# A Mamba round laid out anew on four engines: where the read-outs, the silu calls, the D term and the output product stand

## The chip, the cores and the metric

The kernel runs on one core of a Trainium2 chip. A core has TensorE (PE, matrix products), VectorE (DVE), ScalarE (ACT), GpSimd (POOL) and SyncE (SP), which here issues nearly all transfers. Each engine works through a queue of its own in order, and they wait for one another on semaphores. The metric is the device time of one execution in microseconds (us). Before the change three runs took 8188.65, 8215.14 and 8237.64 us, a median of 8215.14 us.

## What is computed

A decoder of two layers on 64 sequences of 128 tokens with 128 features, in float32. The part that the change touches is the first one, a Mamba model of four layers with 256 inner channels and 16 states each. One layer is, cut to what matters:

```python
hidden = _layernorm(residual, norm_w[i], norm_b[i])
xz = einsum('bld,ed->ble', hidden, in_w)
xin, z = split(xz, 2)
xc = silu(_causal_conv(xin, cw, cb))
dbc = einsum('bld,ed->ble', xc, xp_w)          # dtr (8), Bm (16), Cm (16)
dt = softplus(einsum('blr,dr->bld', dtr, dtp_w) + dtp_b)
# for each token t, from h = 0:
h = exp(dt[t, :, None] * A) * h + (dt[t] * xc[t])[:, None] * Bm[t]
y[t] = einsum('dn,n->d', h, Cm[t])
y = (y + xc * D) * silu(z)
residual = residual + einsum('bld,ed->ble', y, out_w)
...
```

The parts behind it (a cross attention, a layer of experts, a trajectory layer, a decoder layer and a quantized feed-forward layer) run later in the same program and stay as they are.

## The kernel before

`mamba_stage` works in rounds. A round handles four sequences (512 tokens) of one layer; there are 16 rounds a layer and 4 layers. Channels lie on the partitions, in two halves, so a state of one round is a tile of 128 x 1024 (two halves, four sequences, 128 tokens). `round_of` is one round: a block with one queue for each engine, written out by hand, then a barrier at the block's end, then `s.clear()`, in which SP clears all of the stage's semaphores and a second barrier holds all engines. The 16 states n of a round are a pipeline over four engines:

- ScalarE makes the decay factors of state n into PSUM (`act_da`: zeros for each sequence's first token, L347, and two exponentials, L350), one state ahead; PSUM holds them for two states.
- GpSimd makes the products dBu (`pool_dbu`, L365) into a ring of four tiles, three states ahead.
- VectorE runs the recurrence of state n over the tokens (`dve_scan`, L379). For eleven states it then multiplies with C (`dve_read_out`, L393, into `hcd`); for the five states of `ON_POOL` (1, 5, 8, 10, 13) the scan goes into `hs`, and GpSimd multiplies (`pool_read_out`, L402, into `hcp`).
- TensorE adds these products up in two PSUM banks, by a product with the identity (`pe_sum`, L419). The sums begin with the D term (`pe_skip`, L407).

Woven in between are three other things. `Behind` ends the round before: its last sum (L291), the gate with silu(z) on VectorE (L296), the output product with the old residual (L300, L304), and its copy on ScalarE (L310), which SP stores. `Ahead` makes what the next round needs: the conv (L206) and its silu (L212), the x product (L217, copied at L222 and sent through DRAM, so that the B and C rows come back on all partitions), dt (first product L234, Abs and Exp at L239 and L241, a polynomial and a logarithm for softplus, L245 to L260, a second product L234, and VectorE's dt at L265), dtu on GpSimd (L270), and the z product (L275) with its silu (L280). `Pre` normalizes the tokens of the round after that: statistics on VectorE (L166, L169), the addition of eps and the sign (L171, L172), the power -0.5 on GpSimd (L176, L178), the application on ScalarE (L183), transposes on TensorE (L190), and L195.

The order on each engine is set by the text of `round_of` alone: its loops run over n, and an `if n == ...` puts an extra step behind state n. In an engine's queue a wait holds all that stands behind it.

## Time and profile before

| | us |
|---|---|
| median of three runs | 8215.14 (8188.65 to 8237.64) |
| the profiled execution, its own time | 8205.62 |
| span of its profile | 8203.8 |
| Mamba rounds within the span | about 109 to 4090 |
| VectorE busy in them | 3616 |
| GpSimd busy in them | 3349 |

The profile shows one execution. Its times count from the start of the span. Busy time is time in which an engine executes an instruction that computes or loads a table; idle time ahead of an instruction is put down to the engine that released it. TensorE's clock is granted in two levels, 2.4 GHz (1.00) and 1.2 GHz (0.50).

### The profile page before, as it was taken

The page shows a single profiled execution, that of the slowest core. Times are in us where ns is not written, and L with a number is a line of the kernel's source. Part 1 is how long each engine was busy: PE and PEld are TensorE (multiplying, and loading weights), DVE is VectorE, ACT ScalarE, POOL GpSimd, SP SyncE. Part 2 cuts the span into 40 slices and gives each one's busy share as a digit, 9 for nine tenths or more (in the row PEclk, how much of TensorE's full clock was granted, in tenths as well). Part 3 has the DMA queues.
Part 4 walks back from the last instruction along what each step waited for, and adds up shares of the span by engine and source line. Part 5 has one row for each costly group of instructions (what it writes and reads, how often), then busy time and mean ns, then how long its engine had stood idle before and what let it go on. Part 6 is the DMA issues. An engine that isn't in the chain of part 4 may idle for free. (4 is left out here: it accounts for less than half of the span.)

```text
span 8203.8 us, 93492 instructions
## 1 busy us (share of the span) xinstructions
PE 6431.1 (78%) x25989; PEld 3401.5 (41%) x25989; DVE 6477.9 (79%) x15177; ACT 4521.1 (55%) x8427; POOL 4781.6 (58%) x2957
## 2 busy tenths in 40 slices
PE   5888888888888888888788867777557777777855
PEld 2333333333333333333355545555434455555522
DVE  5999989999899998999855668898666666666557
ACT  4666666666666666666555633333324555555533
POOL 4888888888888888888732334455213333343300
PEclk9999999999999999999977878888655777777755
DMA  5333333434333343343310057777310000000011
GB/s 182 144 153 149 153 138 153 161 137 158 152 146 153 148 155 138 153 161 136 148 33 27 22 144 211 210 212 210 92 48 8 10 10 10 10 10 10 7 34 36
DMA packets 373870, 896.58 MB, mean 109 GB/s; under 512 B 28169, under 2 KB 270214, under 8 KB 307110
## 3 DMA queue, kind: packets, MB, share of 16 engines
q1 hardware_dynamic: 332646, 692.64, 22.5%
q0 software_dynamic: 40960, 201.36, 8.4%
q14 instruction: 212, 1.74, 0.1%
q8 instruction: 52, 0.85, 0.0%
HBM read 850.57 MB, written 56.77 MB: 111 GB/s over the span
## 5 line engine op out<-in xcount | busy, mean ns | idle before, releaser
L365 POOL TENSOR_TENSOR mb_dBu<-mb_dtu,mb_rows_b 128x1024 f32<-128x1024 f32 x1027 | 2402.1, 2357 | 145.0 <-POOLq L63 101.1
L379 DVE TENSOR_TENSOR_SCAN mb_bank<-mb_bank,mb_dBu 128x1024 f32<-128x1024 f32 x704 | 1610.9, 2288 | 142.7 <-PEq L63 112.1
L350 ACT ACTIVATE mb_bank<-mb_dt,mb_a_neg 128x508 f32<-128x508 f32 x2050 | 1312.7, 671 | 2.3
L419 PE MATMUL mb_bank<-mb_hcd,ident 128*128 128x512 f32 x2560 | 1211.3, 606 | 29.7 <-DVE mb_hcd L393 29.6
L419 PE MATMUL mb_bank<-mb_hcp,ident 128*128 128x512 f32 x1280 | 860.9, 810 | 345.3 <-POOL mb_hcp L402 345.3
L402 POOL TENSOR_TENSOR mb_hcp<-mb_hs,mb_rows_c 128x1024 f32<-128x1024 f32 x320 | 751.3, 2348 | 478.6 <-DVE mb_hs L379 445.6
L393 DVE TENSOR_TENSOR mb_hcd<-mb_bank,mb_rows_c 128x1024 f32<-128x1024 f32 x704 | 862.1, 1225 | 32.1 <-PE mb_bank L419 0.4
L419 PEld LDWEIGHTS mb_bank<-mb_hcd,ident 128*128 128x128 f32 x2560 | 499.1, 200 | 758.7 <-issue 632.5
L379 DVE TENSOR_TENSOR_SCAN mb_hs<-mb_bank,mb_dBu 128x1024 f32<-128x1024 f32 x320 | 731.1, 2285 | 83.5 <-ACT mb_bank L350 81.7
L1527 POOL DMA_INDIRECT ex_rows<-in_ex_table,ex_idx x512 | 490.0, 957 | 523.5 <-DVE ex_idx L1523 309.7
L419 PEld LDWEIGHTS mb_bank<-mb_hcp,ident 128*128 128x128 f32 x1280 | 306.1, 254 | 779.2 <-POOL mb_hcp L402 413.4
L1020 PE MATMUL de_bank<-ident,de_a_e 128*128 128x128 f32 (+1 forms) x2048 | 373.4, 342 | 213.3 <-DVE de_a_e L1136 213.3
L347 ACT ACTIVATE mb_bank<-mb_zeros 128x8 f32<-128x8 f32 x1025 | 176.1, 172 | 620.4 <-DVE mb_hcd L393 292.6
L206 PE MATMUL mb_bank<-mb_h_ch,mb_w_conv 128*128 128x512 f32 x1040 | 480.6, 604 | 44.0 <-ACT mb_r_post L310 44.0
L977 POOL TENSOR_TENSOR de_a_e<-de_a_sp,de_a_m 128x1024 f32<-128x1024 f32 x128 | 244.9, 1913 | 343.4 <-DVE de_a_m L1122 193.0
L1020 PEld LDWEIGHTS de_bank<-ident,de_a_e 128*128 128x128 f32 (+1 forms) x2048 | 303.8, 182 | 267.2 <-DVE de_a_e L1136 242.3
L1090 ACT ACTIVATE de_a_pt<-de_bank 128x512 f32<-128x512 f32 (+1 forms) x512 | 281.3, 591 | 124.5 <-PE de_bank L1020 124.5
L1611 ACT ACTIVATE ex_dg_in<-ident,ex_lin 128x128 f32<-128x128 f32 x512 | 156.4, 387 | 326.5 <-DVE ex_junk L1638 326.5
L1122 DVE MAX8 de_a_m<-de_a_sp 128x8 f32<-128x128 f32 x1024 | 210.0, 277 | 139.4 <-ACT de_a_sp L1075 69.2
L1504 PE MATMUL ex_bank<-ex_w_sim,ex_xT 128*128 128x512 f32 x512 | 257.7, 646 | 71.1 <-PEq L63 64.4
L206 PEld LDWEIGHTS mb_bank<-mb_h_ch,mb_w_conv 128*128 128x128 f32 x1040 | 194.0, 191 | 282.3 <-issue 226.2
L1581 PE MATMUL ex_bank<-ex_rows,ex_dg_in 128*128 128x256 f32 x1024 | 300.4, 460 | 0.0
(368 smaller groups left out, 12789.3 us busy)
## 6 DMA issues: line engine op xcount, KB each, us to landing
mb_rows_b<-bc_rows SPq DMA_DIRECT2D x259, 1024.0 KB, 7.7
mb_rows_c<-bc_rows SPq DMA_DIRECT2D x258, 1024.0 KB, 6.9
stream<-mb_r_post SPq DMA_DIRECT2D x69, 256.0 KB, 2.6
mb_r_tok<-stream SPq DMA_DIRECT2D x67, 256.0 KB, 2.7
mb_r_old<-stream SPq DMA_DIRECT2D x65, 256.0 KB, 2.8
ex_rows<-in_ex_table,ex_idx POOLq DMA_INDIRECT x512, 5.5
tj_x_tok<-stream SPq DMA_DIRECT2D x17, 256.0 KB, 3.1
bc_rows<-mb_xp SPq DMA_DIRECT2D x65, 64.0 KB, 1.6
```

Source lines behind the costliest of these rows:

```text
L206: m = nc.tensor.matmul(bank[:, M0 + c], w_conv[:, k, c * P:(c + 1) * P], h_ch[:, :, k:k + SEQ], start=(k == 0), stop=(k == DC - 1))
L350: e = nc.scalar.activation(da_of(n)[:, c * GB:(c + 1) * GB, 1:], dt[q][:, c].rearrange("p (b t) -> p b t", b=GB)[:, :, 1:], ACT.Exp, scale ...
L365: nc.gpsimd.tensor_tensor(by_c(dBu[m % RING][:]), by_c(chains(dtu[q][:])), over_c(rows_b[:, n]), ALU.mult).then_inc(s["mb_dbu"], 1)
L379: nc.vector.tensor_tensor_scan(flat(to), flat(da_of(n)), flat(dBu[n % RING][:]), 0.0, ALU.mult, ALU.add).then_inc(s["mb_scan"], 1)
L393: nc.vector.tensor_tensor(by_c(hcd[k % 3][:]), by_c(da_of(n)), over_c(rows_c[:, n]), ALU.mult).then_inc(s["mb_hcd"], 1)
L402: nc.gpsimd.tensor_tensor(by_c(hcp[k % 2][:]), by_c(hs[k % 2][:]), over_c(rows_c[:, n]), ALU.mult).then_inc(s["mb_hcp"], 1)
L419: m = nc.tensor.matmul(bank[:, B_Y + c], ident[:], part[:, c * GB:(c + 1) * GB], start=False, stop=False)
L1020: m = self.nc.tensor.transpose(self.bank[0:nk, 4 + j, h * P:(h + 1) * P], self.e_of(t, nk)[:, 4 * j + h], self.ident[:])
L1090: self.nc.scalar.activation(self.pt[t % 2][0:nk, 4 * j:4 * j + 4].rearrange("p h q -> p (h q)"), self.bank[0:nk, 4 + j], ACT.Copy).then_in ...
L1504: nc.tensor.matmul(bank[:, j], xT[q][:, b], w_sim[:, 4 * j:4 * j + 4], start=True, stop=True).then_inc(p["sim"], 1)
L1527: nc.gpsimd.indirect_dma_start(rowsb[b][:, h], None, w["table"], bass.IndirectOffsetOnAxis(idx[b][:, h:h + 1], 0)).then_inc(got[b], 16)
L1581: m = nc.tensor.matmul(bank[:, HID, 0:FI], dg_in[:, h], rowsb[k % GB][:, h, IB:IB + FI], start=False, stop=(h == PH - 1))
```

## The change

Nothing that is computed changes. In each round the order of the queues is another one:

- Semaphores: there are two sets of them (`Turns`), for even and odd rounds. SP clears the other round's set at the beginning of a round, and `s.clear()` with its barrier goes from the round's end; the block's own barrier stays.
- GpSimd makes dBu two states ahead (`AHEAD`) instead of three, and the round's own first two are made at the end of the round before. A read-out no longer stands directly behind the dBu of its state's turn but where `READ_BEHIND` puts it, behind a dBu.
- VectorE: the gate stands behind scan 1 instead of state 0, the statistics behind state 3 instead of 7, dt behind state 11 instead of 10. L171 and L172 go to ScalarE (`act_var`), behind state 5. The scaled identity for D is made in a layer's first round instead of its last.
- ScalarE: both conv silus and both halves of the z silu stand in one block behind the decay factors made at n = 2. The copy of the output product comes at n = 4.
- TensorE: the D term stands in the middle of the sums; the sums of states 13 and 15 are made at the beginning of the next round (`pe_late_sums`). The conv's first half is made at the end of the round before, the z product stands near the beginning, and the output product behind the x product. The three buffers of `hcd` are taken in the order of `HCD`.

```diff
+AHEAD = 2
+READ_BEHIND = {3: 1, 8: 5, 11: 8, 13: 10, 15: 13}
+HCD = (2, 0, 1, 2, 0, 1, 2, 0, 1, 0, 1)
...
+class Turns:
+    def clear_other(self):
+        for first, end in self.sets[1 - self.q].runs:
+            self.nc.sync.sem_clear(range(first, end))
...
                 for b in range(GB):
-                    nc.vector.bn_aggr(mv[:, b], stats[:, b])
-                dve.drain()
-                nc.vector.tensor_scalar(mv[:, :, 1], mv[:, :, 1], LN_EPS, None, ALU.add)
-                nc.vector.tensor_scalar(shift[:], mv[:, :, 0], -1.0, None, ALU.mult).then_inc(s["mb_stats"], 1)
+                    m = nc.vector.bn_aggr(mv[:, b], stats[:, b])
+                m.then_inc(s["mb_stats"], 1)
...
+            def act_var(self, act):
+                act.wait_ge(s["mb_stats"], self.turn + 1)
+                nc.scalar.activation(shift[:], mv[:, :, 0], ACT.Copy, scale=-1.0)
+                nc.scalar.activation(var[:], mv[:, :, 1], ACT.Identity, bias=eps_at[:, 0:1]).then_inc(s["mb_var"], 1)
...
             def act_z(self, act):
-                act.wait_ge(s["mb_z"], CH)
-                nc.scalar.activation(zg[self.q][:], x_psum, ACT.Silu).then_inc(s["mb_zg"], 1)
+                for c in range(CH):
+                    act.wait_ge(s["mb_z"], c + 1)
+                    nc.scalar.activation(zg[self.q][:, c], bank[:, M0 + c], ACT.Silu).then_inc(s["mb_zg"], 1)
...
-                if j >= 1:
-                    pool.wait_ge(s["mb_scan"], j)
+                if m >= RING:
+                    pool.wait_ge(s["mb_scan"], m - RING + 1)
...
                 @block.gpsimd
                 def _(pool):
-                    for n in range(DS):
-                        scan.pool_dbu(pool, n + RING - 1, n)
-                        if n in ON_POOL:
-                            scan.pool_read_out(pool, n)
-                        if n == 9:
+                    for m in range(AHEAD, DS + AHEAD):
+                        scan.pool_dbu(pool, m)
+                        if m in READ_BEHIND:
+                            scan.pool_read_out(pool, READ_BEHIND[m])
+                        if m == 13:
                             pre.pool(pool)
-                        if n == 11:
+                        if m == 14:
                             ahead.pool_dtu(pool)
...
                         scan.act_da(act, n + 1, n)
-                        if n == 1:
+                        if n == 2:
+                            for c in range(CH):
+                                ahead.act_conv(act, c, 1)
+                            act.wait_ge(s["mb_yg"], 1)
+                            ahead.act_z(act)
+                        if n == 4:
+                            ahead.act_x(act)
                             behind.act_new(act)
-                        if n == 3:
-                            for c in range(CH):
-                                ahead.act_conv(act, c)
                         if n == 5:
-                            ahead.act_x(act)
+                            pre.act_var(act)
...
                         if n == 11:
-                            ahead.act_z(act)
+                            pre.act_tokens(act)
                         if n == 12:
-                            pre.act_tokens(act)
-                        if n == 14:
...
-                        if n == 0:
+                        if n == 1:
                             behind.dve_gate(dve)
-                        if n == 6 and shape == GROUPS - 1:
+                        if n == 6 and shape == 0:
                             dve_skip(dve)
-                        if n == 7:
+                        if n == 3:
                             pre.dve(dve)
...
-                        if n == 10:
+                        if n == 11:
                             ahead.dve_dt(dve)
...
                 @block.tensor
                 def _(pe):
-                    behind.pe_last_sum(pe)
-                    ahead.pe_conv(pe, 0)
-                    behind.pe_out(pe)
...
+                    behind.pe_late_sums(pe)
+                    ahead.pe_conv(pe, 1)
+                    pe.wait_ge(s["mb_yg"], 1)
+                    scan.pe_sum(pe, 0)
+                    ahead.pe_z(pe)
+                    scan.pe_sum(pe, 1)
+                    ahead.pe_x(pe)
+                    behind.pe_out(pe, True)
+                    scan.pe_sum(pe, 2)
+                    scan.pe_sum(pe, 3)
+                    pe.wait_ge(s["mb_new"], 1)
+                    ahead.pe_dt(pe, False)
+                    for n in range(4, 10):
+                        scan.pe_sum(pe, n)
+                    ahead.pe_dt(pe, True)
+                    if shape == 0:
+                        pe.wait_ge(s["mb_skip"], 1)
+                    scan.pe_skip(pe, False)
+                    scan.pe_sum(pe, 10)
+                    scan.pe_sum(pe, 11)
+                    pe.wait_ge(s["mb_dt"], 1)
+                    pre.pe(pe)
+                    scan.pe_sum(pe, 12)
+                    pe.wait_ge(s["mb_h"], 1)
+                    following.pe_conv(pe, 0)
+                    scan.pe_sum(pe, 14)
-            s.clear()
```

GpSimd at the beginning of a round, before: `mb_hcp` is a read-out, `mb_dBu` a product, and `mb_scan` in the brackets a wait for a scan.

```order
L365 TENSOR_TENSOR mb_dBu<-mb_dtu,mb_rows_b 128x1024
L365 TENSOR_TENSOR mb_dBu<-mb_dtu,mb_rows_b 128x1024 [waits mb_scan]
L402 TENSOR_TENSOR mb_hcp<-mb_hs,mb_rows_c 128x1024 [waits mb_scan]
L365 TENSOR_TENSOR mb_dBu<-mb_dtu,mb_rows_b 128x1024 [waits mb_scan] x4
L402 TENSOR_TENSOR mb_hcp<-mb_hs,mb_rows_c 128x1024 [waits mb_scan]
L365 TENSOR_TENSOR mb_dBu<-mb_dtu,mb_rows_b 128x1024 [waits mb_scan] x3
L402 TENSOR_TENSOR mb_hcp<-mb_hs,mb_rows_c 128x1024 [waits mb_sump,mb_scan,mb_c2]
```

The same place of GpSimd's queue after:

```order
L408 TENSOR_TENSOR mb_dBu<-mb_dtu,mb_rows_b 128x1024 x2
L450 TENSOR_TENSOR mb_hcp<-mb_hs,mb_rows_c 128x1024 [waits mb_scan_0]
L408 TENSOR_TENSOR mb_dBu<-mb_dtu,mb_rows_b 128x1024 [waits mb_scan_0] x5
L450 TENSOR_TENSOR mb_hcp<-mb_hs,mb_rows_c 128x1024 [waits mb_late_0,mb_scan_0]
L408 TENSOR_TENSOR mb_dBu<-mb_dtu,mb_rows_b 128x1024 [waits mb_scan_0] x3
L450 TENSOR_TENSOR mb_hcp<-mb_hs,mb_rows_c 128x1024 [waits mb_sump_0,mb_scan_0,mb_c2_0]
```

Two products ahead of the first read-out no longer wait for a scan, and five instead of four stand between the first and the second read-out.

TensorE from the end of a round to the beginning of the next one, before (L419 and L291 are sums, L206 the conv, L300 and L304 the output product; the line with the barrier is the boundary).

```order
L419 MATMUL mb_bank<-mb_hcp,ident 128x512 [waits mb_hcp]
L419 MATMUL mb_bank<-mb_hcp,ident 128x512
L419 MATMUL mb_bank<-mb_hcd,ident 128x512 [waits mb_hcd]
L419 MATMUL mb_bank<-mb_hcd,ident 128x512
L540 UNCONDITIONAL_BRANCH
L642 UNCONDITIONAL_BRANCH [waits barrier_Pool_Activation_PE_DVE_SP_release]
L291 MATMUL mb_bank<-mb_hcd,ident 128x512 x2
L206 MATMUL mb_bank<-mb_h_ch,mb_w_conv 128x512 x4
L300 MATMUL mb_bank<-mb_r_old,ident 128x512 [waits mb_rp]
L304 MATMUL mb_bank<-mb_w_out,mb_yg 128x128 [waits mb_yg]
```

The same place after (L242 is the conv, L467 and L331 are sums, L313 the z product):

```order
L242 MATMUL mb_bank<-mb_h_ch,mb_w_conv 128x512 [waits mb_h_0]
L242 MATMUL mb_bank<-mb_h_ch,mb_w_conv 128x512 x3
L467 MATMUL mb_bank<-mb_hcd,ident 128x512 [waits mb_hcd_0]
L467 MATMUL mb_bank<-mb_hcd,ident 128x512
L594 UNCONDITIONAL_BRANCH
L698 UNCONDITIONAL_BRANCH [waits barrier_Pool_Activation_PE_DVE_SP_release]
L331 MATMUL mb_bank<-mb_hcp,ident 128x512 x2
L331 MATMUL mb_bank<-mb_hcd,ident 128x512 x2
L242 MATMUL mb_bank<-mb_h_ch,mb_w_conv 128x512 x4
L467 MATMUL mb_bank<-mb_hcd,ident 128x512 [waits mb_hcd_1,mb_yg_1]
L467 MATMUL mb_bank<-mb_hcd,ident 128x512
L313 MATMUL mb_bank<-mb_h_ch,mb_w_z 128x512 [waits mb_u_1] x2
```

The sum of a GpSimd read-out has moved from ahead of the boundary to behind it, one conv the other way, and the z product stands where the output product stood.

ScalarE around the silu calls, before (L347 and L350 are the decay factors of a state, L212 the conv's silu, L222 the copy of the x product).

```order
L347 ACTIVATE mb_bank<-mb_zeros 128x8 [waits mb_hcd]
L350 ACTIVATE mb_bank<-mb_dt,mb_a_neg 128x4x127 x2
L212 ACT_TABLE_LOAD
L212 ACTIVATE mb_u<-mb_bank,mb_conv_b 128x512 [waits mb_conv] x2
L347 ACTIVATE mb_bank<-mb_zeros 128x8 [waits mb_hcd]
L350 ACT_TABLE_LOAD
L350 ACTIVATE mb_bank<-mb_dt,mb_a_neg 128x4x127 x2
```

The same place after (L390 and L393 are the decay factors, L249 the conv's silu, L319 that of z):

```order
L390 ACTIVATE mb_bank<-mb_zeros 128x8 [waits mb_scan_1]
L393 ACTIVATE mb_bank<-mb_dt,mb_a_neg 128x4x127 x2
L249 ACT_TABLE_LOAD
L249 ACTIVATE mb_u<-mb_bank,mb_conv_b 128x512
L249 ACTIVATE mb_u<-mb_bank,mb_conv_b 128x512 [waits mb_conv_1]
L319 ACTIVATE mb_zg<-mb_bank 128x512 [waits mb_z_1,mb_yg_1]
L319 ACTIVATE mb_zg<-mb_bank 128x512 [waits mb_z_1]
L390 ACTIVATE mb_bank<-mb_zeros 128x8 [waits mb_hcd_1]
L393 ACT_TABLE_LOAD
L393 ACTIVATE mb_bank<-mb_dt,mb_a_neg 128x4x127 x2
```

The z silu, with its waits for the z product and for the gate, now stands between the conv's silu and the decay factors of state 4.

## Rows read from the trace of the kernel before

**Rows 1.** The page, busy tenths of VectorE in 40 slices of the span:

```profile
DVE  5999989999899998999855668898666666666557
```

**Rows 2.** Table by stretch (us; busy and count of PE, PEld, DVE, ACT, POOL; clock; DMA):

```profile
1537.09:1598.86 61.77, 53.31 (x122) 22.41 (x122) 56.05 (x42) 40.37 (x70) 52.44 (x25) 0.92 0.38 150
...
1598.86:1660.00 61.14, 53.13 (x123) 22.43 (x123) 56.04 (x42) 40.21 (x70) 52.20 (x25) 0.92 0.38 151
...
109.00:4090.00 3981.00, 3404.73 (x7818) 1427.21 (x7819) 3616.15 (x2665) 2579.93 (x4424) 3348.87 (x1536) 0.92 0.38 150
```

**Rows 3.** Groups, 100 to 4100 us: count | busy us, mean ns | idle before, releasers:

```profile
L365 POOL TENSOR_TENSOR mb_dBu<-mb_dtu,mb_rows_b 128x1024 f32<-128x1024 f32 x1027 | 2402.1, 2357 | 145.0 <-POOLq L63 101.1 <-DVE mb_bank L379 41.9
...
L379 DVE TENSOR_TENSOR_SCAN mb_bank<-mb_bank,mb_dBu 128x1024 f32<-128x1024 f32 x704 | 1610.9, 2288 | 142.7 <-PEq L63 112.1 <-ACT mb_bank L350 19.0 <-issue 11.1
...
L350 ACT ACTIVATE mb_bank<-mb_dt,mb_a_neg 128x508 f32<-128x508 f32 x2050 | 1312.7, 671 | 2.3
...
L379 DVE TENSOR_TENSOR_SCAN mb_hs<-mb_bank,mb_dBu 128x1024 f32<-128x1024 f32 x320 | 731.1, 2285 | 83.5 <-ACT mb_bank L350 81.7 <-issue 1.8
...
L350 ACT ACT_TABLE_LOAD x193 | 247.6, 1283 | 0.9
...
L265 DVE SCALAR_TENSOR_TENSOR mb_dt<-mb_bank,mb_ln 128x1024 f32<-128x1024 f32 x64 | 78.4, 1225 | 102.3 <-PE mb_bank L234 102.3
...
L171 DVE TENSOR_SCALAR mb_mv<-mb_mv 128x4 f32<-128x4 f32 x64 | 47.6, 743 | 5.3
```

**Rows 4.** Timeline of VectorE: start, us, engine, line, operation [idle before, releaser]:

```profile
1565.04 0.91 DVE L171 TENSOR_SCALAR mb_mv<-mb_mv 128x4 f32<-128x4 f32 x1
...
1567.22 2.29 DVE L379 TENSOR_TENSOR_SCAN mb_hs<-mb_bank,mb_dBu 128x1024 f32<-128x1024 f32 x1 [1.21 <-ACT mb_bank L350]
...
1579.50 1.23 DVE L265 SCALAR_TENSOR_TENSOR mb_dt<-mb_bank,mb_ln 128x1024 f32<-128x1024 f32 x1 [1.56 <-PE mb_bank L234]
...
1580.64 2.29 DVE L379 TENSOR_TENSOR_SCAN mb_bank<-mb_bank,mb_dBu 128x1024 f32<-128x1024 f32 x1
...
1584.10 2.29 DVE L379 TENSOR_TENSOR_SCAN mb_bank<-mb_bank,mb_dBu 128x1024 f32<-128x1024 f32 x1
...
1595.68 1.23 DVE L393 TENSOR_TENSOR mb_hcd<-mb_bank,mb_rows_c 128x1024 f32<-128x1024 f32 x1
...
1598.86 2.30 DVE L379 TENSOR_TENSOR_SCAN mb_bank<-mb_bank,mb_dBu 128x1024 f32<-128x1024 f32 x1 [1.96 <-PEq L63]
...
1602.33 1.21 DVE L296 TENSOR_TENSOR mb_yg<-mb_zg,mb_bank 128x1024 f32<-128x1024 f32 x1
...
1603.46 2.28 DVE L379 TENSOR_TENSOR_SCAN mb_hs<-mb_bank,mb_dBu 128x1024 f32<-128x1024 f32 x1
...
1605.66 2.27 DVE L379 TENSOR_TENSOR_SCAN mb_bank<-mb_bank,mb_dBu 128x1024 f32<-128x1024 f32 x1
```

**Rows 5.** Timeline of GpSimd, same columns:

```profile
1569.65 2.35 POOL L402 TENSOR_TENSOR mb_hcp<-mb_hs,mb_rows_c 128x1024 f32<-128x1024 f32 x1 [3.73 <-DVE mb_hs L379]
...
1574.27 1.01 POOL L176 TENSOR_TENSOR mb_rstd<-mb_mv,minus_half 128x4 f32<-128x4 f32 x1
...
1592.34 4.67 POOL L365 TENSOR_TENSOR mb_dBu<-mb_dtu,mb_rows_b 128x1024 f32<-128x1024 f32 x2
```

**Rows 6.** Timeline of ScalarE, the conv's silu:

```profile
1548.87 1.28 ACT L212 ACT_TABLE_LOAD   x1
...
1550.16 1.26 ACT L212 ACTIVATE mb_u<-mb_bank,mb_conv_b 128x512 f32<-128x512 f32 x2
```

**Rows 7.** Timeline of TensorE at two boundaries between rounds:

```profile
1537.09 1.95 PE L291 MATMUL mb_bank<-mb_hcd,ident 128*128 128x512 f32 x4 [0.70 <-PEq L63]
...
1595.91 1.88 PE L419 MATMUL mb_bank<-mb_hcd,ident 128*128 128x512 f32 x4
```

**Rows 8.** Table by stretch, columns as in rows 2, on both sides of a clock step:

```profile
1592.40:1595.80 3.40, 3.36 (x4) 1.51 (x5) 3.37 (x3) 1.39 (x3) 3.40 (x2) 0.50 0.00 0
...
1595.80:1633.30 37.50, 33.35 (x87) 14.22 (x85) 33.66 (x29) 22.13 (x38) 28.62 (x13) 1.00 0.53 211
```

139 lines of the change are left out of this document (78 added, 61 removed).

## The prediction

> **What bounds the kernel now.** I read the profile from the outside in. The slices of the page show VectorE at nine tenths or more in nearly all of the first twenty of forty slices, and lower behind them [rows 1]; that first half is the Mamba stage, and the change touches nothing else. The table by stretch then gives the stage: from 109 to 4090 us VectorE is busy 3616 of 3981 us, GpSimd 3349, TensorE 3405, ScalarE 2580 [rows 2]. The dt product of VectorE (L265) stands 64 times in the groups, so the stage is 64 rounds [rows 3]; a round takes 61.8 or 61.1 us in turn (the longer one ends in the loop's branch), 61.45 in the mean [rows 2]. VectorE is thus the bound, with 365 us of idle time, and what a change here can give is that idle time plus whatever work it takes off VectorE. The groups name who ended the idle time: 112.1 us at the boundary between rounds, 102.3 us in which dt waits for TensorE's second dt product (L234), 81.7 and 19.0 us in which a scan waits for ScalarE's decay factors (L350) [rows 3]. The timeline of VectorE shows the same in one round: 1.21 us ahead of the scan behind the statistics, 1.56 us ahead of dt, 1.96 us at the boundary [rows 4].
>
> **The change part by part.** All of it is worked out for one round of VectorE and then times 64, against the profiled execution (8205.6 us; its span is 8203.8, and it lies 9.5 us under the median of the three runs).
>
> *The eps addition and the sign go to ScalarE.* L171 works on 128x4 numbers and still takes 743 ns in the mean [rows 3]; in the round shown it occupies 0.91 us [rows 4]. With L172 behind it VectorE loses about 0.9 us a round: 58 us in all. ScalarE gets two tiny instructions instead; between nothing (it waits there for work) and 0.5 us each, the length of one of its small instructions, and I take 0.4 us for both, in time in which ScalarE waits for VectorE anyway. Until now this term was half hidden, because a wait for ScalarE followed it [rows 4]; both have to go for it to count. The Trainium skill speaks against this move: its page "ScalarE: Activation LUTs" (Rules for kernel authors) says that additions and multiplications belong on VectorE, which does them faster. By that page the move would be worth nothing or less; the row differs: four columns take 743 ns where a read-out of 1024 columns takes 1230 [rows 3, 4], so what costs here isn't the arithmetic, and the measurement decides.
>
> *dt's wait.* Before, VectorE asks for dt behind scan 10, after, behind scan 11 and its read-out, 3.46 us later (the distance of two scans that each have a read-out [rows 4]). On TensorE the second dt product no longer stands with the z product behind it, and the sum ahead of it that waits longest, that of state 8, is fed earlier: GpSimd's read-out of state 8, which waited 3.73 us for its scan [rows 5], now stands behind three more products of dBu. Counting from the round's first scan, TensorE ends the dt product near 39 us at full clock and 40 us with one stretch at half clock, VectorE asks for it at 41.9. The 102 us go, and nothing takes their place up to a delay of 1.9 us.
>
> *The scans' waits for ScalarE.* The 1.21 us came about because ScalarE's Abs waited for TensorE's first dt product. That product now stands behind sum 3 instead of sum 4. Of the six table loads a round (193 at L350 are three a round, and one each at L212, L249, L280) two go, because the conv silu and the z silu share one: 2 x 1.28 us of ScalarE [rows 3, 6]. The walk that decides: decay factors of state 4 must be there when VectorE comes to scan 4, at 15.3 us (two pairs and more: pair 3.46, scan without read-out 2.20, gate 1.13, pair, pair, statistics 1.4 [rows 4]). Ahead of them ScalarE now has, from 7.3 us: a load 1.28, two silus 0.63 each, two more of z, a load 1.28 [rows 6], and the decay factors, 1.42 (two of 0.67 that overlap a little, and the zeros ahead of them [rows 3]). The z silus wait for TensorE: two late sums of 1.72, conv 3.44, sum 0, then z, 11.2 us at full clock. That gives 14.7 us against 15.3: 0.6 us of slack. The 101 us go. Here ScalarE is in order, so all decay factors behind the block and with them VectorE wait if z is late.
>
> *The boundary.* Before, TensorE comes last: its sums 13 and 14 start only with GpSimd's last read-out, and the last one starts at 1595.91, 0.2 us behind VectorE's last read-out, and ends 1.9 us later [rows 4, 7]. Its own wait there is 0.70 us where no branch follows, two barriers with a clearing of semaphores between them [rows 7]. After, sums 13 and 15 are made in the next round and one barrier and the clearing leave the path. Half of 0.70 remains, and about 0.35 more each second time for the branch: 0.5 in the mean. GpSimd's queue becomes the last to arrive: 16 products, 5 read-outs and dtu at 2.33 (two in 4.67 [rows 5]) and the norm at 1.2 (1.01 and a small one) make 52.5 us; walked through, it waits 1.2 us for scan 1, 1.2 for scan 5 and 1.0 for scan 10, and ends at 56.1, where VectorE ends at 55.8. So the boundary costs VectorE 0.5 + 0.3 = 0.8 us instead of 1.8: 64 us less.
>
> *New waits.* No row of before shows TensorE starting a round with 10 us of work that ScalarE's block needs. From below it costs nothing (0.6 us of slack). From above: TensorE now stands idle for about 2 us at the boundary, and where it idled so before, it then ran at half clock: granted 0.50 in 1592.4 to 1595.8, behind a wait for GpSimd's read-out, and 1.00 for 37.5 us from the boundary on [rows 8]. One such stretch makes TensorE 1.7 us late. If it falls whole on the start of the round, 0.3 to 1.1 us reach VectorE; two of them, 2.0 us. I take 0.6 us a round, nearer to the lower end, because TensorE's queue is at full clock in 37.5 of 61.4 us before: 38 us. Below nothing is excluded, as no other wait is named.
>
> *At nothing.* The product of D (skip) is two of TensorE's 1.72 us, moved to where TensorE waits for GpSimd; its scaled identity moves from a layer's last round to its first, the same VectorE time. The output product is later, its store still 30 us ahead of the round's end. The row loads keep their places, and their waits on dBu counts are shifted by what was shifted. At the program's start four memsets of a state-sized tile come in (at most 5 us, by the 1.23 of a read-out of that size [rows 4]) and two table loads go (2.6 us).
>
> The sum: 58 + 102 + 101 + 64 - 38 = 287 us less, 8205.6 - 287 = 7919, about 7920. Per round that is 57.0 us. As a test of the floor: 61.77 less the waits of that round (5.1) and L171 (0.9) is 55.8, and 0.8 and 0.6 on top are 57.2.
>
> **The rivals.** *All waits vanish:* no new wait and the boundary at 0.5: 8205.6 - 58 - 102 - 101 - 83 = 7862. For it speaks the slack found above at every step but scan 4; against it that every handed-over result so far cost a few tenths somewhere (19.0 us in 64 rounds at one scan [rows 3]). *GpSimd becomes the bound:* it already ends last by 0.3 us with 3.4 us of waits inside. Each of its read-outs behind a scan that VectorE delivers late pushes all dBu behind it, and VectorE can't go on without these. If 1.5 us a round come to that, 96 us come back: 8015. For it speaks that its busy time is 52.4 us of a round [rows 2]; against it that its products stand 5 to 9 us ahead of their scans in the walk from scan 4 to scan 13, and 3 us at scan 15. *The silu block holds ScalarE:* as a table load that costs more than its row, the block delays scan 4. With 2.6 us a switch, two switches in the block make scan 4 2.0 us late, 128 us in all: 8050. The trace puts the next instruction 1.29 us behind the load's start [rows 6], so I give this little. By the Trainium skill, page "ScalarE: Activation LUTs" (What ACT_TABLE_LOAD costs), a switch is 1283 ns and a drain of 1380 ns; the first half agrees with the row, the second isn't seen in it. *Slower:* half clock through the start of the round. Until z there are 10.3 us of TensorE's work at full clock; at half clock all through, z ends at 21 us, the decay factors of state 4 at 24, and VectorE waits 8.8 us at scan 4: a round of 65.4, 4 us over today's, 8460. It decides from a wait of 4.5 us on, that is with three half-clock stretches one after another at the start of each round; the row of before has one such stretch and then 37.5 us at full clock [rows 8], and what came before it was a wait for a read-out, a kind that the change shortens. *It doesn't do what it says:* a new last comer at the barrier (a late row load, TensorE's conv of the next round) eats most of it, 8190.
>
> **How the numbers follow.** The forecast as worked out, 7880 to 7980: 0.60. All waits vanish, to 7860: 0.17. GpSimd, 7980 to 8040: 0.11. The silu block: 0.03. Nothing gained: 0.04. Slower: 0.05. The range 7855 to 8040 holds the first three and leaves out about 0.15. About 0.5% (41 us) is what a measurement of this kernel tells from no change: faster by more than that 0.91, within it 0.04, slower 0.05.
>
> **What would show it.** In the profile after: VectorE's group of dt without a wait for TensorE; the scans' waits for ScalarE under 40 us in total, and at scan 4 if anywhere; the boundary's group near 50 us instead of 112; rounds of 56.5 to 57.5 us; four table loads a round; GpSimd's read-outs waiting about 1 us instead of 2 to 4. It would be wrong if the granted clock sat at half over the boundary, if dBu took the place of the decay factors as what scans wait for, or if VectorE's read-outs waited for sums.

## The result, and the profile after

The changed kernel takes 7863.22 us (median of five runs, 7847.71 to 7916.4), the kernel before 8215.14 us (five runs, 8188.65 to 8239.94): a ratio of 0.9582, with a 95% interval of 0.9549 to 0.9615. The forecast was 7920, in a range from 7855 to 8040. The profiled execution of after is the longest of its five, 7916.4 us; that is 289 us under the profiled one of before, and nearly the 287 us forecast, but by chance, as the next rows show.

The table by stretch of both kernels, each cut at the first and last instruction of three stages (us from the span's start and length; busy time and number of instructions of PE, PEld, DVE, ACT, POOL; granted clock; DMA share and GB/s). First before:

```profile
46.20:4092.20 4046.00, 3430.94 (x7874) 1438.05 (x7874) 3632.48 (x2707) 2603.01 (x4455) 3360.54 (x1544) 0.92 0.38 149
4095.40:4765.50 670.10, 570.42 (x4608) 370.77 (x4608) 381.46 (x1237) 370.81 (x768) 194.74 (x240) 0.78 0.10 27
6133.70:7856.30 1722.60, 1315.10 (x9152) 843.34 (x9152) 1115.01 (x4904) 961.89 (x1615) 643.71 (x528) 0.74 0.03 10
```

Then after:

```profile
46.00:3767.50 3721.50, 3277.68 (x7886) 1364.31 (x7886) 3542.41 (x2580) 2477.18 (x4523) 3356.28 (x1543) 0.96 0.43 162
3770.80:4500.70 729.90, 631.31 (x4608) 410.03 (x4608) 380.75 (x1237) 372.35 (x768) 194.96 (x240) 0.70 0.09 25
5869.00:7568.00 1699.00, 1291.21 (x9152) 828.36 (x9152) 1115.69 (x4904) 961.28 (x1615) 647.30 (x528) 0.75 0.03 10
```

The first row of each is the Mamba stage, the only one that the change touches: 4046.0 to 3721.5, 324.5 us less. The other two stages have the same instructions before and after. The first of them (prefix xa in the trace) got 59.8 us longer at a granted clock of 0.70 instead of 0.78, and the other (de) 23.6 us shorter. In all the profiles of this study, with that code always the same, xa took 650 to 741 us and de 1679 to 1743, and all that lies outside the Mamba stage took 4133 to 4230. So the whole time of one run says little below 1%, and the experiments are read by the Mamba stage, from one profile of each kernel. Its length is steady: a second profile of the changed kernel gave 3720.9.

Between the first scan and the end of the last round, the rounds take this long (same columns, before and after):

```profile
109.30:4083.90 3974.60, 3401.43 (x7808) 1425.69 (x7808) 3613.73 (x2664) 2579.91 (x4424) 3348.14 (x1536) 0.92 0.38 150
```

```profile
117.80:3757.60 3639.80, 3242.50 (x7808) 1349.40 (x7808) 3521.48 (x2535) 2454.29 (x4488) 3345.21 (x1536) 0.96 0.43 164
```

That is 62.10 us a round before and 56.87 after, in the mean over all 64; rounds at the beginning and the end of a layer are longer than the others, before and after. VectorE's idle time fell from 360.9 to 118.3 us, its busy time by 92.2. The groups of VectorE after (columns as in [rows 3]) tell which waits went:

```profile
L422 DVE TENSOR_TENSOR_SCAN mb_bank<-mb_bank,mb_dBu 128x1024 f32<-128x1024 f32 x704 | 1608.3, 2284 | 92.4 <-PEq L594 49.7 <-ACT mb_bank L393 18.0 <-PEq L507 13.7
L422 DVE TENSOR_TENSOR_SCAN mb_hs<-mb_bank,mb_dBu 128x1024 f32<-128x1024 f32 x320 | 729.4, 2279 | 0.0
...
L495 DVE TENSOR_SCALAR mb_skip<-ident,mb_vec 128x128 f32<-128x128 f32 x8 | 10.3, 1326 | 0.0
```

Against [rows 3]: the boundary (<-PEq) 112.1 to 49.7 us; the scans' waits for ScalarE 81.7 + 19.0 to 18.0, all at scan 4 and in 32 of the 64 rounds; dt, 102.3 before, waits no more inside a round; and the pair L171 and L172 is gone. The 13.7 us stand once, ahead of the first round.

### The profile page after: what moved, and what is told of

Same layout as the page of the kernel before. It is cut to its first block and busy times, and to the rows that moved or that the text cites. A ratio compares the mean times of both kernels' runs of the same rounds, so it can differ in the third digit from the quotient of the medians.

```text
span 7914.6 us, 93170 instructions
## 1 busy us (share of the span) xinstructions
PE 6312.7 (80%) x26001; PEld 3351.6 (42%) x26001; DVE 6387.3 (81%) x15050; ACT 4396.2 (56%) x8495; POOL 4780.0 (60%) x2956
## 5 line engine op out<-in xcount | busy, mean ns | idle before, releaser
L422 DVE TENSOR_TENSOR_SCAN mb_bank<-mb_bank,mb_dBu 128x1024 f32<-128x1024 f32 x704 | 1608.3, 2284 | 92.4 <-PEq L594 49.7
L467 PE MATMUL mb_bank<-mb_hcd,ident 128*128 128x512 f32 x2560 | 1232.1, 612 | 100.5 <-DVE mb_hcd L439 94.1
L393 ACT ACTIVATE mb_bank<-mb_dt,mb_a_neg 128x508 f32<-128x508 f32 x2050 | 1311.2, 670 | 1.5
L450 POOL TENSOR_TENSOR mb_hcp<-mb_hs,mb_rows_c 128x1024 f32<-128x1024 f32 x320 | 753.6, 2355 | 220.7 <-DVE mb_hs L422 220.7
L467 PEld LDWEIGHTS mb_bank<-mb_hcd,ident 128*128 128x128 f32 x2560 | 475.6, 195 | 755.8 <-issue 513.2
L467 PE MATMUL mb_bank<-mb_hcp,ident 128*128 128x512 f32 x1024 | 549.3, 663 | 141.9 <-POOL mb_hcp L450 141.2
L390 ACT ACTIVATE mb_bank<-mb_zeros 128x8 f32<-128x8 f32 x1025 | 176.0, 172 | 750.7 <-DVE mb_hcd L439 326.0
L242 PE MATMUL mb_bank<-mb_h_ch,mb_w_conv 128*128 128x512 f32 x1048 | 474.1, 594 | 0.9 <-ACT mb_h_ch L231 0.9
L467 PEld LDWEIGHTS mb_bank<-mb_hcp,ident 128*128 128x128 f32 x1024 | 200.6, 203 | 434.8 <-issue 221.9
L242 PEld LDWEIGHTS mb_bank<-mb_h_ch,mb_w_conv 128*128 128x128 f32 x1048 | 198.7, 190 | 256.8 <-issue 255.5
```

What stands on the lines that cost most here:

```text
L242: m = nc.tensor.matmul(bank[:, M0 + c], w_conv[:, k, c * P:(c + 1) * P], h_ch[:, :, k:k + SEQ], start=(k == 0), stop=(k == DC - 1))
L393: e = nc.scalar.activation(da_of(n)[:, c * GB:(c + 1) * GB, 1:], dt[q][:, c].rearrange("p (b t) -> p b t", b=GB)[:, :, 1:], ACT.Exp, scale ...
L422: nc.vector.tensor_tensor_scan(flat(to), flat(da_of(n)), flat(dBu[n % RING][:]), 0.0, ALU.mult, ALU.add).then_inc(s["mb_scan"], 1)
L450: nc.gpsimd.tensor_tensor(by_c(hcp[(k + self.q) % 2][:]), by_c(hs[k % 2][:]), over_c(rows_c[:, n]), ALU.mult).then_inc(s["mb_hcp"], 1)
L467: m = nc.tensor.matmul(bank[:, B_Y + c], ident[:], part[:, c * GB:(c + 1) * GB], start=(n == 0), stop=False)
```

## Where it shows in one round

VectorE's timeline after, at two boundaries and one scan 4 (start us, us, engine, line, operation, out<-in, count [idle before, releaser]); it answers [rows 4]:

```profile
1538.13 2.30 DVE L422 TENSOR_TENSOR_SCAN mb_bank<-mb_bank,mb_dBu 128x1024 f32<-128x1024 f32 x1 [0.69 <-PEq L594]
1540.46 1.23 DVE L439 TENSOR_TENSOR mb_hcd<-mb_bank,mb_rows_c 128x1024 f32<-128x1024 f32 x1
1541.60 2.28 DVE L422 TENSOR_TENSOR_SCAN mb_hs<-mb_bank,mb_dBu 128x1024 f32<-128x1024 f32 x1
...
1594.22 2.30 DVE L422 TENSOR_TENSOR_SCAN mb_bank<-mb_bank,mb_dBu 128x1024 f32<-128x1024 f32 x1 [1.04 <-PEq L594]
...
1609.84 2.30 DVE L422 TENSOR_TENSOR_SCAN mb_bank<-mb_bank,mb_dBu 128x1024 f32<-128x1024 f32 x1 [0.59 <-ACT mb_bank L393]
```

The boundary is 0.69 us without the loop's branch and 1.04 with it, instead of 1.51 and 1.96. TensorE at the same two boundaries, which answers [rows 7]:

```profile
1538.14 1.96 PE L331 MATMUL mb_bank<-mb_hcp,ident 128*128 128x512 f32 x4 [2.12 <-PEq L594]
```

```profile
1594.27 3.65 PE L331 MATMUL mb_bank<-mb_hcp,ident 128*128 128x512 f32 x4 [2.52 <-PEq L594]
```

The first late sum takes 1.96 us in one round and 3.65 in the other: the second time TensorE had been idle for 2.52 us, and in 1594.20 to 1597.60 the granted clock is 0.51 (1.2 GHz), in the stretch before it 1.00. In that round z is late and scan 4 waits 0.59 us for the decay factors that stand behind the silu block; in the other it doesn't wait. So it is in all 64 rounds: where scan 4 waits, the granted clock of the round's first 11 us is 0.84 or 0.85 in the mean (32 rounds), where it doesn't, it is 1.00 (31 rounds) or 0.90 (one). ScalarE's block in the undisturbed round, which answers [rows 6]:

```profile
1545.33 1.28 ACT L249 ACT_TABLE_LOAD   x1
1546.62 1.27 ACT L249 ACTIVATE mb_u<-mb_bank,mb_conv_b 128x512 f32<-128x512 f32 x2
1548.59 0.60 ACT L319 ACTIVATE mb_zg<-mb_bank 128x512 f32<-128x512 f32 x1 [0.70 <-PE mb_bank L313]
1549.38 0.60 ACT L319 ACTIVATE mb_zg<-mb_bank 128x512 f32<-128x512 f32 x1 [0.20 <-PE mb_bank L313]
1549.88 0.17 ACT L390 ACTIVATE mb_bank<-mb_zeros 128x8 f32<-128x8 f32 x1
1550.06 1.28 ACT L393 ACT_TABLE_LOAD   x1
1551.35 1.29 ACT L393 ACTIVATE mb_bank<-mb_dt,mb_a_neg 128x508 f32<-128x508 f32 x2
```

One load serves both silus, and the instruction behind a load starts 1.29 us after the load's start, so no second half of a switch is to be seen. Four loads a round are left (two of them at L393), of six. GpSimd's five read-outs (L450) wait 1.17, 0.97, 0, 0.91 and 0 us in the round from 1538 us on, where one of them waited 3.73 before [rows 5]; their group of the stage shows 220.7 us of idle time, 478.6 before.

## The experiments

The theory: VectorE is still the bound, and each wait went through the part of the change that the prediction names for it. The rivals differ by part, and stand with each run. Lengths are those of the Mamba stage, against 3721.5 for the changed kernel. Each run is the changed kernel with one edit, where nothing else is said. A ratio, where one is given, is that of the whole time to the kernel before; the runs without one were executed once.

**One barrier back.** At the end of each round:

```diff
+            nc.all_engine_barrier()
```

> The changed kernel with the second barrier put back at the end of every round; the late sums and all else stay. My theory: the boundary's gain has two parts, the sums and read-outs that no longer arrive last and one barrier that left the path. A barrier with its clearing took 0.37 to 0.40 us in the trace of before, so the Mamba stretch gets 0.37 x 64 = 24 us longer (15 to 35), the round 56.8 instead of 56.4 us, and the boundary's group at the first scan goes from 50 to about 74 us. Rival, the gain at the boundary came from the late sums alone and the barrier hides behind other arrivals: 0 us, within 5.

Measured: 3747.0, 25.5 us longer. The boundary's group (the release at L726):

```profile
L422 DVE TENSOR_TENSOR_SCAN mb_bank<-mb_bank,mb_dBu 128x1024 f32<-128x1024 f32 x704 | 1608.5, 2285 | 115.6 <-PEq L726 69.0 <-ACT mb_bank L393 21.2 <-PEq L507 13.3
```

49.7 became 69.0; 3 us more are waits for ScalarE and 2 lie behind the last round. The barrier doesn't hide: the first scan of a round comes 0.73 us behind the last instruction of the round before it, 0.40 in the changed kernel and 0.79 in the kernel before (means; the clearing stays away in this run). So of the 62.4 us that the boundary gave, some 0.33 x 64 = 21 are the second barrier and 4 what went with it, the clearing for one. The rest is the last arriver: TensorE ended 0.9 us behind VectorE before, and GpSimd ends 0.33 us behind it after (55.7 and 56.0 us from the round's first scan). The ratio to before is 0.9668 [0.964, 0.9696].

**One late sum instead of two.**

```diff
-LATE = 2
+LATE = 1
...
+                    scan.pe_sum(pe, 13)
```

(the added line stands ahead of sum 14 at the end of the round)

> The changed kernel with one late sum instead of two: sum 13 is made at the end of its own round again, sum 15 still in the next one. My theory: TensorE ends at 55.3 us in the walk, still before GpSimd's 56.1, so the boundary doesn't get longer, while the z product in the next round comes 1.7 us sooner and the waits at scan 4 for ScalarE's decay factors (18 us in all) vanish: 0 to -18 us in the Mamba stretch. Rival, it was the taking away of both sums that bought the boundary: with sum 13 back TensorE is the last to arrive, about 0.9 us a round and +60 us, the boundary's group back at 110 us.

Measured: 3703.4, 18.1 us less, a ratio of 0.9527 [0.9498, 0.9556]:

```profile
L422 DVE TENSOR_TENSOR_SCAN mb_bank<-mb_bank,mb_dBu 128x1024 f32<-128x1024 f32 x704 | 1607.2, 2283 | 78.6 <-PEq L594 49.8 <-PEq L507 13.8 <-issue 11.4
```

The boundary stays at 49.8 us; only one of the two sums had to leave it. The waits for ScalarE are gone from the row's three largest (3.5 us at scan 4 in three rounds are left, of 18.0 in 32). So the new wait of the changed kernel comes with TensorE's second late sum. Two things went with that sum, and the run doesn't part them: its own 1.7 us ahead of z, as the prediction's walk has it, and the half clock. With sum 13 back TensorE is idle 0.9 us at a boundary instead of 2.1 (medians), and the granted clock of a round's first 11 us is 1.00 in 61 of 64 rounds. The three others (0.72 to 0.84, each the first round of a layer) are the ones that wait. For the clock speaks that with both sums, too, no round at full clock waits.

**The eps pair back on VectorE.** The two calls of act_var go, and behind bn_aggr:

```diff
+                dve.drain()
+                nc.vector.tensor_scalar(mv[:, :, 1], mv[:, :, 1], LN_EPS, None, ALU.add)
+                nc.vector.tensor_scalar(shift[:], mv[:, :, 0], -1.0, None, ALU.mult).then_inc(s["mb_stats"], 1)
```

> The changed kernel with the addition of eps and the sign of the mean back on VectorE, two instructions on 128x4 numbers; ScalarE's two small ones go. My theory, that VectorE is still the bound and nothing behind these two waits any more: all of 0.9 us a round comes back, 0.9 x 64 = 58 us (50 to 65), rounds of 57.3 us, and the two instructions take 0.6 to 0.9 us each although they hold four columns a partition. Rival, GpSimd is the bound now (it ended 0.3 us behind VectorE in the walk) and VectorE's term hides in its own slack: under 20 us.

Measured: 3861.7, 140.2 us longer, a ratio of 0.9772 [0.9722, 0.9821]. Neither theory gave that. The two instructions take 160.4 us, and the 18.0 us of waits at scan 4 are gone. The group, and one round of VectorE and GpSimd:

```profile
L204 DVE TENSOR_SCALAR mb_mv<-mb_mv 128x4 f32<-128x4 f32 x64 | 150.4, 2350 | 5.8 <-issue 1.2
...
L205 DVE TENSOR_SCALAR mb_shift<-mb_mv 128x4 f32<-128x4 f32 x64 | 10.0, 156 | 0.0
```

```profile
1549.59 2.37 DVE L204 TENSOR_SCALAR mb_mv<-mb_mv 128x4 f32<-128x4 f32 x1
```

```profile
1542.63 9.29 POOL L410 TENSOR_TENSOR mb_dBu<-mb_dtu,mb_rows_b 128x1024 f32<-128x1024 f32 x4
```

GpSimd's four products end at 1551.92, VectorE's addition of four columns at 1551.96. The last of the four (2.3 us each) began as the addition did, and the addition lasts as long as that product. In all 64 rounds it ends 0.023 to 0.031 us behind the end of a GpSimd product. The kernel before shows the same once one looks for it. Its row of GpSimd ahead of the addition of [rows 4]:

```profile
1558.93 6.99 POOL L365 TENSOR_TENSOR mb_dBu<-mb_dtu,mb_rows_b 128x1024 f32<-128x1024 f32 x3
```

These products end at 1565.92, L171 at 1565.95. In 52 rounds of before it took 0.80 to 0.92 us and ended so; in the other 12 it took 0.17, with no product running. It cost less than now because it came later into the product (1.48 to 1.58 us behind its start), and GpSimd then stood waiting for its scan [rows 5]. That is what the Trainium skill says on its page "SBUF — State Buffer" (Who interferes with whom): VectorE and GpSimd share a pair of SBUF ports, which the instruction that issues first holds to its end; a tensor_scalar can need the pair, a tensor_reduce on this chip never does. The next run tests it.

**Two small sums more.** The changed kernel with ScalarE's pair as it is, and besides:

```diff
+                dve.drain()
+                nc.vector.tensor_reduce(spare[:, 0:GB], mv[:, :, 0:2], AX.X, ALU.add)
+                nc.vector.tensor_reduce(spare[:, GB:], mv[:, :, 0:2], AX.X, ALU.add).then_inc(s["mb_stats"], 1)
```

> The changed kernel with two small instructions more on VectorE, at the place where the run with eps on VectorE had its own two: each adds up the eight statistics of a partition in pairs into a spare tile that nobody reads; ScalarE still makes the eps addition and the sign. In the run with eps on VectorE the first of the two took 2350 ns in the mean and ended 0.03 us behind the end of a GpSimd product, and the Mamba stretch got 140 us longer instead of 58. My theory now: what costs there is neither the arithmetic nor an instruction more, but that this form (one SBUF input, a plain addition of a number) can't run while GpSimd has an instruction in progress; a sum along the row isn't held up like that, so these two take some 0.17 us each and the Mamba stretch gets 0.3 to 0.5 us a round, 20 to 32 us, longer, with no group of VectorE above 0.3 us for them. Rival: any instruction on four columns behind the statistics pays for a drain of the pipeline or for GpSimd, whatever its form: 58 to 140 us more.

Measured: 3733.9, 12.4 us longer, less than either expected:

```profile
L205 DVE TENSOR_REDUCE mb_spare<-mb_mv 128x4 f32<-128x8 f32 x64 | 10.3, 161 | 5.6 <-issue 1.2
...
L206 DVE TENSOR_REDUCE mb_spare<-mb_mv 128x4 f32<-128x8 f32 x64 | 9.7, 151 | 0.0
```

161 ns stand against 2350 at the same place behind the same statistics, with the same kind of drain, and a GpSimd product was running at each of the 64. So neither the place nor the small size costs; the form does, by what GpSimd happens to run. That the addition wrote back into the tile that it read isn't the reason: a scaling from one tile into another was lengthened in the same way (2.37 us, below). (Of the 20 us of work, some 10 are taken from the wait at scan 4, which fell from 18.0 to 8.2 us.)

**The eps pair alone.** The kernel before, with eps and the sign on ScalarE (the call of act_var behind act_log) and nothing else changed.

> The kernel before with one part of the change alone: eps and the sign on ScalarE, all else as it was. My theory: this part alone gives little, because in most rounds of before the scan behind the statistics waits for ScalarE's decay factors anyway (81.7 us at the hs scans), and that wait grows by the 0.9 us that VectorE comes sooner: 0 to -15 us, the wait for ScalarE up from 81.7 to 120 to 140 us. Rival, the parts add up one by one: -58 us, the wait as it was.

Measured: 4066.6 against 4046.0 of before: no gain at all, and 20.6 us longer. (The ratio of the whole times is 1.0065 [1.0044, 1.0086], 53 us; what of it lies outside the Mamba stage is code that is the same.)

```profile
L383 DVE TENSOR_TENSOR_SCAN mb_hs<-mb_bank,mb_dBu 128x1024 f32<-128x1024 f32 x320 | 730.8, 2284 | 156.0 <-ACT mb_bank L354 156.0
```

```profile
1570.47 2.29 DVE L383 TENSOR_TENSOR_SCAN mb_hs<-mb_bank,mb_dBu 128x1024 f32<-128x1024 f32 x1 [2.27 <-ACT mb_bank L354]
```

The wait of scan 8, 1.21 us in [rows 4], is now 2.27: what VectorE saves it spends waiting for ScalarE, whose Abs still waits for TensorE's first dt product. The waits grew by 74 us at the hs scans and 12 at the others, more than the 58 saved; dt's wait fell by 25, the boundary's rose by 17. Rounds of one of the four layers ran at 62.2 and 64.2 us in turn, the others as before; why that layer did is open. Over a layer's first fifteen rounds three layers took what they took before within 1 us, and this one 17.6 us more. So the edit alone is worth nothing, and the loss on top is not explained.

**dt one scan earlier.** Its condition goes from n == 11 back to n == 10.

> The changed kernel with VectorE's dt product one scan earlier, behind scan 10, where it stood before. My theory: of the 102 us of dt's wait a part went through TensorE's earlier dt product and the rest through the later place; by the walk TensorE ends the second dt product 0.3 us (full clock) to 1.7 us (half clock at the round's start) behind the point at which VectorE asks for it, so a wait for TensorE stands at dt again and the Mamba stretch gets 20 to 110 us longer. Rival, the later place isn't needed, TensorE's order alone removed the wait: 0 us, within 10.

Measured: 3814.7, 93.2 us longer:

```profile
L303 DVE SCALAR_TENSOR_TENSOR mb_dt<-mb_bank,mb_ln 128x1024 f32<-128x1024 f32 x64 | 78.4, 1225 | 111.4 <-PE mb_bank L272 111.4
```

The whole wait of before is back (111.4, 102.3 in [rows 3]), 1.74 us a round. TensorE's new order did bring dt earlier: it ends the second product 39.7 us behind the round's first scan, 42.2 before. But VectorE itself is earlier by more: it comes to this place at 37.8 us, 40.9 before (medians). In the changed kernel it asks at 41.9, so the later place removed the wait.

**z late again.** TensorE makes z behind dt, ScalarE its silus at n == 11:

```diff
-                            act.wait_ge(s["mb_yg"], 1)
-                            ahead.act_z(act)
...
+                            ahead.act_z(act)
...
-                    ahead.pe_z(pe)
...
+                    ahead.pe_z(pe)
+                    pe.wait_ge(s["mb_zg"], CH)
```

> The changed kernel with the z product late again: TensorE makes it behind dt and ScalarE its two silus ahead of the next round's norm, with a table load of their own; all else stays. My theory, from the walk of TensorE's queue: with two late sums at the round's start there is no room behind dt, the conv and the state sums behind z come late, and scan 13 and the boundary wait, about 5 us a round, +350 us (200 to 400) in the Mamba stretch: the z product's new place, not the silu table loads, is what the move rests on. Rival: the block's worth is two table loads of ScalarE, which has 1100 us of idle time in this stretch, so 0 to 20 us.

(The x product and the output product no longer wait for the z silus.)

Measured: 4054.2, 332.7 us longer, the whole gain and a little more:

```profile
L423 DVE TENSOR_TENSOR_SCAN mb_hs<-mb_bank,mb_dBu 128x1024 f32<-128x1024 f32 x320 | 730.0, 2281 | 358.2 <-ACT mb_bank L394 358.2
```

All 358.2 us stand at scan 13, 5.6 a round. ScalarE waits there for z ahead of decay factors that are due; one round of ScalarE and of TensorE:

```profile
1647.64 1.28 ACT L320 ACT_TABLE_LOAD   x1
1654.34 0.60 ACT L320 ACTIVATE mb_zg<-mb_bank 128x512 f32<-128x512 f32 x1 [5.41 <-PE mb_bank L314]
```

```profile
1653.28 1.88 PE L314 MATMUL mb_bank<-mb_h_ch,mb_w_z 128*128 128x512 f32 x4
```

The load was done 5.41 us before z came, so the two table loads that the block saves are not what it is for (the second, behind the silus, is on the way with its 1.28 us); the place of z on TensorE is. In this run z stands behind the D term and the sums 10 and 11, and began 2.5 us behind the end of VectorE's dt (1650.78). That no late place would do is not shown: z directly behind dt, as in the kernel before, wasn't run with the new order. The parts can't be taken one by one.

**Three read-outs earlier.**

```diff
-READ_BEHIND = {3: 1, 8: 5, 11: 8, 13: 10, 15: 13}
+READ_BEHIND = {3: 1, 7: 5, 10: 8, 12: 10, 15: 13}
```

(The text ahead of the run names the states 8, 11 and 13; the products of these numbers moved, the read-outs are those of states 5, 8 and 10.)

> The changed kernel with three of GpSimd's five read-outs put one product earlier again: those of states 8, 11 and 13, where they stood before. My theory: GpSimd then waits 1.5 to 3 us for these scans as it did before, every product behind them is late, and GpSimd becomes the last to arrive: by the walk it ends at 58.5 us of a round instead of 56.1, so rounds of 58.7 us and about +147 us (100 to 180) in the Mamba stretch; the new idle time of VectorE stands at scans that wait for GpSimd's dBu and at the boundary. Rival, GpSimd has slack for it and the place of the read-outs matters only for TensorE's sum ahead of dt: 0 to 20 us.

Measured: 3920.4, 198.9 us longer:

```profile
L450 POOL TENSOR_TENSOR mb_hcp<-mb_hs,mb_rows_c 128x1024 f32<-128x1024 f32 x320 | 753.0, 2353 | 461.3 <-DVE mb_hs L422 410.8 <-issue 50.5
```

```profile
L422 DVE TENSOR_TENSOR_SCAN mb_bank<-mb_bank,mb_dBu 128x1024 f32<-128x1024 f32 x704 | 1608.7, 2285 | 187.3 <-PEq L594 128.5 <-ACT mb_bank L393 30.0 <-issue 15.0
L422 DVE TENSOR_TENSOR_SCAN mb_hs<-mb_bank,mb_dBu 128x1024 f32<-128x1024 f32 x320 | 730.0, 2281 | 57.0 <-ACT mb_bank L393 57.0
```

GpSimd's read-outs wait 461 us again and the boundary costs 128.5, more than before the change. The direction is the theory's; GpSimd ends 58.4 us behind the round's first scan, as the walk had it (58.5), but the size is a third above the walk's 147. VectorE's waits stand at the boundary and at decay factors (scan 13: 57.0), not at scans that wait for dBu as expected. The row of ScalarE ahead of those decay factors tells why:

```profile
L219 ACT ACTIVATE mb_xh<-mb_r_tok,mb_shift,mb_rstd 128x128 f32<-128x128 f32 x259 | 106.7, 482 | 294.6 <-POOL mb_shift L209 294.6
```

In ScalarE's queue the normalization of the tokens stands ahead of the decay factors of state 13, and it waits for the norm that a late GpSimd makes (L209): 294.6 us, 146.2 in the changed kernel.

**Better versions.** On top of one late sum, one memset ahead of the first round instead of five (only VectorE's last tile is read by the one late sum of the first round), and then VectorE's work for a new layer on ScalarE too:

```diff
+        def act_layer(act):
+            for c in range(CH):
+                nc.scalar.activation(w_out[:, c], out_raw[:, c], ACT.Copy)
+            for c in range(CH):
+                m = nc.scalar.activation(skip[:, c], ident[:], ACT.Identity, scale=vec[:, DD + c:DD + c + 1])
+            m.then_inc(s["mb_skip"], 1)
```

(called behind act_exp in a layer's first round, where VectorE had its copy and its two scalings). They ran beside the changed kernel:

> The changed kernel itself once more, as the measure for the two others of this call. Expected by every theory: the Mamba stretch within 3 us of the 3721.5 us of its first profile; the other stages are the same code in all runs and move with the granted clock of their first stage by up to 70 us, so the whole time may differ by 0.5%.

> The changed kernel with one late sum instead of two (as in the run above, which took 18 us off the Mamba stretch) and with one memset of a state-sized tile ahead of the first round instead of five, since only the last of VectorE's tiles is then read by the first late sum. Theory: -18 us of the late sum, and 4 memsets of 0.91 us on the way to the first round, -4 us: -22 us (15 to 26) in the Mamba stretch. Rival, the memsets lie beside the first loads: -18 us as before.

> As the run with one late sum and one memset, and besides with VectorE's two instructions of a new layer on ScalarE: the scaling of the identity by D (two of 128x128 numbers) and the copy of the output weights. In the trace of the changed kernel the first of the two scalings takes 2375 ns in every layer and the second 274, so the first stands 2.1 us for GpSimd's product; the copy takes 1540. Theory, VectorE the bound in these four rounds too: 4 x (2.65 + 1.54) = 17 us less in the Mamba stretch than the run with one late sum and one memset (10 to 18), 40 us less than the changed kernel. Rival, ScalarE is late there (four instructions of some 0.3 us ahead of its decay factors) or another engine bounds these rounds: 0 to -5 us.

| kernel | Mamba stage, us | median, us | ratio to before |
|---|---|---|---|
| the changed kernel again | 3720.9 | 7886.06 | 0.9598 [0.957, 0.9627] |
| one late sum, one memset | 3700.8 | 7865.52 | 0.9585 [0.9554, 0.9617] |
| the same, layer's work on ScalarE | 3683.4 | 7809.35 | 0.9498 [0.9472, 0.9524] |

The memsets bring 2.6 us of the 4 expected against the run with one late sum (3703.4); the first scan comes 5.7 us sooner in the stage, and why the rounds behind it gave half of that back is open. The layer's work brings 17.4: in a layer's first round VectorE's first scaling took 2.37 us for 128 columns and the second 0.27; on ScalarE the four instructions take 0.29 to 0.39 us each, though a GpSimd product was running each time. The last kernel is the fastest of the study, 38 us under the changed one in the Mamba stage; the rest of the difference of the medians lies in stages whose code is the same.

## Why the prediction was right, and where it was off

The bound was right: VectorE's idle time and the work taken off it are the whole gain, and of the rivals none came as a mechanism. A table load costs ScalarE the 1.28 us of its row and no more, and GpSimd ends last by 0.33 us (the walk had 0.3: 56.1 against 55.8 us, measured 56.0 against 55.7) and did not become the bound; the run with three read-outs earlier shows what that would have been. The walk of dt held too: the product ends at 39.7 us (39 to 40 forecast), VectorE asks at 41.9.

The time itself was met less well than the mechanism. 7863 lies 8 us inside the lower end of the range and below the 7880 to 7980 to which the prediction gave 0.60, in a gap up from 7860 to which it gave no chance. It is the figure of the rival in which all waits vanish (7862), by luck: 18 us of new waits and 49.7 us at the boundary are left where that rival has 0 and 32, and gains that no step named make up for them.

The terms, forecast and as the rows give them, over the Mamba stage:

| step | forecast, us | measured, us |
|---|---|---|
| eps and sign off VectorE | -58 | -57.7 (L171 and L172 gone) |
| dt's wait | -102 | -102.3 |
| scans' waits for ScalarE | -101 | -100.7 |
| boundary | -64 | -62.4 (112.1 to 49.7) |
| new waits | +38 | +18.0 (all at scan 4) |
| scaled identity (skip), moved | 0 | -4.8 (1922 to 1326 ns, eight times) |
| ahead of the first scan | at most +5, -2.6 | +8.5 (109.3 to 117.8) |
| behind the last round | 0 | +1.5 |
| what is left | 0 | -25 |
| sum | -287 | -324.5 |

*New waits* is the mis-sized step. The mechanism and the place were right: half clock on TensorE ahead of z, felt at scan 4. It took 0.6 us in every round; measured are 0.56 us in 32 of 64, because the half-clock stretch falls on z's way only in these; why it does so in one of two like rounds is open. (The terms that the prediction lists for VectorE's way to scan 4 add up to 15.1 us, not 15.3, and measured are 15.0; the decay factors are there at 14.5 at full clock, 14.7 forecast.)

*What is left* is the other miss: it had no step. About 30 us of VectorE's lower busy time belong to no removed instruction. Where an instruction doesn't wait, it starts before the one ahead of it has ended (1541.60 against 1540.46 + 1.23 = 1541.69 in the timeline above), so a wait that goes brings these 0.09 us besides. 248 waits of scans and dt above 0.1 us, those at the boundary left out, became 32; by that row an estimate of 216 x 0.09 = 19 us. The rest isn't settled.

*Ahead of the first scan:* the memsets were counted, the first round's conv that TensorE now makes ahead of the first barrier was not; VectorE waits 13.7 us there, 10.5 before.

The sum stayed 37 us short in the Mamba stage, and the median 57 under the forecast; the other 20 must lie in the stages that didn't change, as the Mamba stage is steady, but the median execution itself wasn't profiled.

*Readings that were wrong.* The step on dt has the read-out of state 8 behind three more products; by the order of GpSimd's queue it is one more in the round (ten instead of nine). In the round shown its wait is gone all the same. The step on new waits has TensorE at full clock in 37.5 us of a round; by the mean of 0.92 in [rows 2] an estimate is 51 of 61.4. And the three chances that the range holds add up to 0.88, which leaves out 0.12 and not 0.15.

*One sentence stood on an incomplete reason.* The prediction put the price of L171 on something other than arithmetic and left it there. As a term against before, 58 us was right. As the worth of the edit it was not: alone it is worth nothing (the wait behind it takes it), and with the rest of the change it is worth 140, since GpSimd now has a product running where it stood waiting before. The forecast held because it priced all edits at once along VectorE's path and required that the wait behind L171 go too. That the change takes half of the waits from GpSimd's read-outs, and so makes such a pair on VectorE dearer, no step said.

Of what the prediction named as signs these came as named: no wait at dt, 18 us for ScalarE and only at scan 4, a boundary group of 49.7, four table loads a round, read-outs that wait about 1 us. One sign did not: rounds of 56.5 to 57.5 us. The mean of all rounds, 56.87, would fit, but the forecast started from the 61.45 us of ordinary rounds, and these take 55.7 and 56.8 in turn, or 56.1 and 56.4: 56.25.

## What to carry to other kernels

Price the edits of such a change together, along the bound engine, and ask of each what stands late behind it: here the same pair of instructions took 58 us in its rows, moving it alone gained nothing, and moving it back cost 140 us once the rest had been moved. A tiny instruction with a long mean duration may be waiting inside its row; set its end against the ends of the engine it may share something with before moving it. When work is moved off a boundary, move only what arrives last: one of two late sums bought the whole boundary, and the second left TensorE idle there, with a half-clock stretch behind it in half of the rounds, and cost 18 us.

## What the hardware showed that was not expected

An addition on 128x4 numbers on VectorE took 0.17, 0.9 or 2.36 us in different arrangements of the same work; in 52 rounds of before and in all 64 of the run with eps on VectorE it ended 0.023 to 0.031 us behind the GpSimd product that was running. Sums along the row at the same place took 0.16. A scaling of 128x128 took 2.37 us and its twin right behind it 0.27. No group of waits shows this time: it counts as busy.
